# Two of four parts of the difference tables ahead of the first relu, products on plain tables first, and state stores ahead of weights, in the second layer of a graph network

## The reference, cut to what matters

```python
def conv(h, W, b):
    h = h @ W
    agg = jax.ops.segment_sum(h[src] * norm, dst, num_segments=n)
    return agg + b
h = jnp.maximum(_layernorm(x, axis=-1), 0.0)
h = jax.nn.relu(conv(h, W1, b1))
h = jax.nn.relu(conv(h, W2, b2))          # the "second layer" of the title
x = x + conv(h, W3, b3)
h = jnp.maximum(_layernorm(x, axis=-1), 0.0)
msg = h[edge_src] + relvectors[edge_rel]
red = jax.ops.segment_sum(msg, edge_dst, num_segments=h.shape[0])
x = x + _gru_cell(red, h, w_ih, w_hh, b_ih, b_hh)
```

## Time and profile before

| | |
|---|---|
| median of three runs | 869.26 us |
| the profiled execution | 868.13 us, of which its span is 864.0 us |
| mean granted TensorE clock | 0.987 of full |
| PE busy | 823.6 us (95%) |
| DVE, ACT, POOL busy | 606.2, 297.5 and 117.0 us |

### The profile page before, as it was taken

How to read it: one execution, slowest core, us unless ns; L and a number is a source line. 1 busy time by engine, 2 the same in 40 slices (tenths; PEclk the granted TensorE clock), 3 DMA queues, 4 the chain that set the end, 5 groups by cost and what they waited for, 6 DMA issues and landing times.

```text
span 864.0 us, 14285 instructions
## 1 busy us (share of the span) xinstructions
PE 823.6 (95%) x4710; PEld 466.9 (54%) x4710; DVE 606.2 (70%) x1319; ACT 297.5 (34%) x604; POOL 117.0 (14%) x244
## 2 busy tenths in 40 slices
PE   2889999999999996999999999999999999999997
PEld 1357566666666444455545545555554555455554
DVE  8945999999999277253869546575664746565677
ACT  3365666776766222110101212221302122112233
POOL 0210110012000046555730000000000000000000
PEclk9889999999999998999999999999999999999999
DMA  6100000000000512332111112222705112111232
GB/s 205 33 2 1 4 18 23 17 17 17 24 17 17 172 38 76 111 75 75 40 35 55 53 55 85 74 86 79 214 3 163 32 42 51 31 36 42 57 79 53
DMA packets 83769, 49.83 MB, mean 58 GB/s; under 512 B 46667, under 2 KB 80220, under 8 KB 83692
## 3 DMA queue, kind: packets, MB, share of 16 engines
q1 hardware_dynamic: 73836, 39.00, 16.1%
q10 hardware_dynamic: 9856, 9.85, 3.6%
HBM read 29.68 MB, written 18.78 MB: 56 GB/s over the span
## 4 chain that ended last, share of the span: by engine, by line
PE 83%; DVE 11%; issue 2%; DMA 2%; ACT 1%; SPq 1%; ACTq 0%; DVEq 0%
PE ps L1396 16%; PE ps L1058 13%; PE ps L1743 9%; PE ps L1570 8%; PE ps L955 8%; PE ps L757 5%; PE ps L764 5%; PE ps L1421 5%; PE ps L1439 3%; PE ps L769 2%; PE ps L774 2%; PE ps L1030 2%; DVE node_b L298 1%; DVE count L598 1%; PE ps L986 1%
## 5 line engine op out<-in xcount | busy, mean ns | idle before, releaser
L1058 PE MATMUL ps<-node_a,count 128*128 128x512 f16 x525 | 181.1, 381 | 1.5 <-DVE node_a L1165 1.0
L955 PE MATMUL ps<-node_b 128*128 128x175 f16 x808 | 162.3, 256 | 6.7 <-DVE node_b L298 5.3
L298 DVE TENSOR_TENSOR node_b<-node_b 128x1024 f16<-128x1024 f16 (+2 forms) x253 | 157.3, 670 | 0.0
L1254 ACT ACTIVATE count<-ps 128x500 f32 x202 | 122.8, 608 | 65.2 <-PE ps L955 59.5
L1396 PE MATMUL ps<-count,node_a 128*128 128x512 f16 (+2 forms) x686 | 130.7, 351 | 0.0
L955 PEld LDWEIGHTS ps<-node_b 128*128 128x128 f16 x808 | 79.5, 100 | 36.0 <-issue 6.2
L2327 POOL TENSOR_TENSOR count<-count,node_a 16x20 f16 x202 | 86.1, 426 | 92.8 <-DMA chapter_starts<-in_dst 52.3
L1396 PEld LDWEIGHTS ps<-count,node_a 128*128 128x128 f16 (+1 forms) x686 | 60.1, 98 | 69.1 <-issue 0.4
L1743 PE MATMUL ps<-count,node_a 128*128 128x512 f16 x288 | 64.1, 379 | 0.0
L1058 PEld LDWEIGHTS ps<-node_a,count 128*128 128x128 f16 x525 | 53.2, 101 | 18.9 <-ACT count L1254 1.2
L1701 DVE TENSOR_TENSOR count<-count 128x6144 f16<-128x6144 f16 x14 | 46.9, 3353 | 17.6 <-PE ps L1570 16.3
(11 more groups left out here) (289 smaller groups left out, 1137.2 us busy)
## 6 DMA issues: line engine op xcount, KB each, us to landing
node_a<-second_scratch ACTq DMA_DIRECT2D x6, 768.0 KB, 4.3
node_a<-in_x SPq DMA_DIRECT2D x4, 768.0 KB, 8.4
second_scratch<-node_a ACTq DMA_DIRECT2D x4, 768.0 KB, 3.5
state_scratch<-params SPq DMA_DIRECT2D x24, 128.0 KB, 1.9
node_b<-state_scratch SPq DMA_DIRECT2D x96, 32.0 KB, 2.1
table_scratch<-agg SPq DMA_DIRECT2D x21, 128.0 KB, 1.8
mixed_scratch<-node_b SPq DMA_DIRECT2D x10, 256.0 KB, 2.0
node_a<-mixed_scratch SPq DMA_DIRECT2D x4, 640.0 KB, 6.8
```

The lines of the kernel that those rows point to most:

```text
L298: return DVE.tensor_tensor(to, iota, keys.unsqueeze(2).to_broadcast([P, n, width, 2]), ALU.is_equal)
L955: return PE.matmul(window(s)[:, :, keys], low, key_hot[k][:, j, :, i].rearrange("p (t w) -> p t w", w=SPAN), start=(s == 0 and j == 0), st ...
L1058: last = PE.matmul(out_slot(u)[0:m, :], count[:, t, u * P:u * P + m], node_a[:, t, :, :].rearrange("p a d -> p (a d)"), start=(t == 0), st ...
L1254: ACTE.activation(to, window(s), ACT.Copy).then_inc(win_written, 1)
```

## The change

It has three pieces. In the second layer, two of the four parts of the difference tables are made before the first relu of chunk 0 and two after it (before: three and one), and the step s1 of pair 2 moves behind the relu of chunk 6. A pair's products come in the order B21, B11, T1, T4, T2, B22, T3, with T4 in bank 3 and the separate tail in bank 0; DVE makes s4 right after s2, both after T1, and in pair 2 the steps y, a12 and a21 of pair 1 come ahead of c11 and s2. Tables are placed and loaded otherwise: four go into `node_b`, where two did. At the end of the third layer, SP stores the state of the last chunk's first two tiles ahead of its wait and of the loads of weights.

```diff
-        SECOND_PRODUCTS = (T1, B21, B11, T4, T2, B22, T3)
-        TAKEN, ADDED = ("t1", "c11", "c21"), ("c11", "c12", "tail", "b22", "c21", "c22")
+        SECOND_PRODUCTS = (B21, B11, T1, T4, T2, B22, T3)
+        TAKEN, ADDED = ("c11", "t1", "c21"), ("c11", "c12", "tail", "b22", "c21", "c22")
@@ second_place @@
-            if p == 1:
-                return slot(SLOT_P if which in (T1, T2) else SLOT_Q)
-            if which in (T1, T2):
+            if (p, which) in ((1, T1), (1, T3), (2, T4)):
                 return slot(SLOT_P)
-            f = 1 if which == T4 else 0
-            return node_b[:, 0:T - 1:2, :, f * P:(f + 1) * P]
+            if (p, which) == (1, T4):
+                return slot(SLOT_Q)
+            odd, f = (1, 0) if (p, which) == (2, T2) else (0, 1)
+            return node_b[:, odd:T - 1:2, :, f * P:(f + 1) * P]
...
-        SECOND_BANK = {T1: 0, T4: 0, B21: 1, B22: 1, B11: 2, T2: 2, T3: 2}
-        TAIL_SUMS = 3
+        SECOND_BANK = {T1: 0, T4: 3, B21: 1, B22: 1, B11: 2, T2: 2, T3: 2}
+        TAIL_SUMS = 0
@@ second_sums_pe @@
-            PE.wait_ge(*SECOND_IN[p, T1])
-            PE.wait_ge(*second_step_at("s1", p))
             if p == 1:
-                PE.wait_ge(sums_out, 4)
+                PE.wait_ge(sums_out, 5)
             else:
-                PE.wait_ge(*second_taken_at(p - 1, "c21"))
-            second_product_pe(p, T1, True, None).then_inc(product_done, 1)
+                PE.wait_ge(*second_added_at(p - 1, "b22"))
+            second_product_pe(p, B21, True, (0, 0)).then_inc(product_done, 1)
             if p == 1:
                 convs_pe(1, 0, 2)
             else:
                 half_convs_pe(p - 1, 1)
-                PE.wait_ge(*second_added_at(p - 1, "b22"))
-            second_product_pe(p, B21, True, (0, 0)).then_inc(product_done, 1)
+            second_product_pe(p, B11, True, None).then_inc(product_done, 1)
+            PE.wait_ge(*SECOND_IN[p, T1])
+            PE.wait_ge(*second_step_at("s1", p))
             if p > 1:
-                PE.wait_ge(*second_added_at(p - 1, "c22"))
-            second_product_pe(p, B11, True, None).then_inc(product_done, 1)
-            second_tail_pe(p, ps[:, TAIL_SUMS, :], 1, 1, True)
+                PE.wait_ge(*second_added_at(p - 1, "tail"))
+            second_product_pe(p, T1, True, None).then_inc(product_done, 1)
             PE.wait_ge(*SECOND_IN[p, T4])
+            if p > 1:
+                PE.wait_ge(*second_taken_at(p - 1, "c21"))
+            second_product_pe(p, T4, True, (0, 1))
             PE.wait_ge(*second_taken_at(p, "t1"))
-            second_product_pe(p, T4, True, (0, 1)).then_inc(product_done, 1)
+            second_tail_pe(p, ps[:, TAIL_SUMS, :], 1, 1, True).then_inc(product_done, 1)
@@ layers_dve @@
-            for b in range(2):
-                parts_dve(b)
-                second_step_dve("s1", b + 1)
-                parts_low_dve(b)
-            parts_dve(2)
-            parts_low_dve(2)
-            relu_chunk(PLAIN[0])
-            parts_dve(3)
-            parts_low_dve(3)
-            relu_chunk(PLAIN[1])
+            parts_dve(0)
+            second_step_dve("s1", 1)
+            parts_low_dve(0)
+            parts_dve(1)
+            parts_low_dve(1)
+            relu_chunk(PLAIN[0])
+            for b in (2, 3):
+                parts_dve(b)
+                parts_low_dve(b)
+            relu_chunk(PLAIN[1])
+            second_step_dve("s1", 2)
             for p in PAIRS_OUT:
+                relu_chunk(PLAIN[2] if p == 1 else 2 * p - 1)
+                if p == 2:
+                    for which in ("y", "a12", "a21"):
+                        second_step_dve(which, 1)
+                second_add_dve(p, "c11")
                 second_step_dve("s2", p)
-                relu_chunk(PLAIN[2] if p == 1 else 2 * p - 1)
                 second_step_dve("s4", p)
...
@@ layers_act @@
-            for b in (1, 2):
-                parts_high_act(b)
-                parts_store_act(b)
+            parts_high_act(1)
+            parts_store_act(1)
             sums_of(0, 1)
             highs(PLAIN[0])
             for f in range(HALVES):
                 sums_of(1, f)
-            parts_high_act(3)
-            parts_store_act(3)
+            for b in (2, 3):
+                parts_high_act(b)
+                parts_store_act(b)
             sums_of(2, 0)
...
@@ layers_sp @@
+            for t in tiles_of[chunks[-1]][:2]:
+                state_store_sp(order, place[t])
             SP.wait_ge(*product_at(0, B22))
             SP.wait_ge(*step_at(0, "s3"))
             gru_weights_sp()
...
-            for t in tiles_of[chunks[-1]]:
+            for t in tiles_of[chunks[-1]][2:]:
                 state_store_sp(order, place[t])
```

More of the change, by code:

```diff
@@ L1510, in program @@
         PLAIN, PAIRS_OUT = chunks[:3], (1, 2)
-        SECOND_PRODUCTS = (T1, B21, B11, T4, T2, B22, T3)
-        TAKEN, ADDED = ("t1", "c11", "c21"), ("c11", "c12", "tail", "b22", "c21", "c22")
-        SECOND_STEPS = [("s1", 1), ("s1", 2), ("s2", 1), ("s4", 1), ("s3", 1), ("s2", 2), ("s4", 2), ("y", 1), ("a12", 1), ("a21", 1),
+        SECOND_PRODUCTS = (B21, B11, T1, T4, T2, B22, T3)
+        TAKEN, ADDED = ("c11", "t1", "c21"), ("c11", "c12", "tail", "b22", "c21", "c22")
+        SECOND_STEPS = [("s1", 1), ("s1", 2), ("s2", 1), ("s4", 1), ("s3", 1), ("y", 1), ("a12", 1), ("a21", 1), ("s2", 2), ("s4", 2),
                         ("s3", 2), ("y", 2), ("a12", 2), ("a21", 2)]
@@ L1541, in second_table @@
             return second_place(p, which)[:, i, part, :]
-        SECOND_IN = {(1, T1): (nodes_in[0], 32), (1, T2): (nodes_in[0], 48), (2, T1): (nodes_in[0], 64), (2, T2): (nodes_in[0], 80),
-                     (1, T4): (nodes_in[1], 32), (1, T3): (nodes_in[1], 48), (2, T4): (nodes_in[2], 48), (2, T3): (nodes_in[3], 48)}
+        SECOND_IN = {(1, T1): (nodes_in[0], 32), (1, T3): (nodes_in[0], 48), (2, T4): (nodes_in[0], 64), (1, T4): (nodes_in[1], 32),
+                     (1, T2): (nodes_in[2], 48), (2, T1): (nodes_in[2], 80), (2, T3): (nodes_in[2], 112), (2, T2): (nodes_in[3], 48)}
         PART_ORDER = (T1, T3, T4, T2)
@@ L1669, in second_load_act @@
             of = second_dram[PART_ORDER.index(which), :, :].rearrange("p (i a d) -> p i a d", a=2, d=P)
-            if (p, which) in ((2, T4), (2, T3)):
+            if SECOND_IN[p, which][0] in nodes_in[2:]:
                 for part in range(2):
@@ L1697, in second_step_dve @@
             else:
-                DVE.wait_ge(*second_product_at(p, {"s2": T1, "s4": B21, "s3": T2}.get(which, T3)))
+                DVE.wait_ge(*second_product_at(p, {"s2": T1, "s4": T1, "s3": T2}.get(which, T3)))
             if n:
@@ L2148, in layers_act @@
             sums_of(2, 1)
-            second_load_act(2, T4)
+            second_load_act(1, T2)
             for p in PAIRS_OUT:
-                second_take_act(p, "t1")
-                second_load_act(p, T2)
-                highs(PLAIN[2] if p == 1 else 2 * p - 1)
                 second_take_act(p, "c11")
                 if p == 2:
-                    ACTE.wait_ge(*second_product_at(p, B11))
-                    second_load_act(p, T3)
+                    second_load_act(p, T2)
+                highs(PLAIN[2] if p == 1 else 2 * p - 1)
+                second_take_act(p, "t1")
+                second_load_act(p, T3)
                 second_take_act(p, "c21")
                 if p == 1:
-                    second_load_act(p, T3)
                     ACTE.wait_ge(*second_product_at(p, T2))
                     second_load_act(p + 1, T1)
+                    ACTE.wait_ge(*second_product_at(p, T3))
+                    second_load_act(p + 1, T4)
                 highs(2 * p)
```

## The result

The changed kernel takes 857.81 us (median of four, 857.42 to 858.21); before, it is 868.6 us (median of four, 866.5 to 869.59). The ratio is 0.9879, with a 95% interval of 0.9858 to 0.9900: 1.2% faster. The forecast was 859.2 us. The profiled execution took 857.42 us, with a span of 853.2 us against 864.0.

A forecast was written before the change was run, and what follows sets the result against it. PE, busy 95%, was taken as the bound, with two waits from 300 to 700 us. Gains 6.80 + 2.08 + 1.86 less a new 0.70 wait make 10.04 us off the 869.26 median: 859.2 us, range 857.6 to 862.8.

The forecast's parts named there:

- The wait for `agg`: Before the second layer's first convs: PE no longer waits for ACT's copy of the second sum, gain 6.80 us.
- The convs' clock: First 16 convs: without idle time PE's clock stays up, 3.45 us instead of 5.53, gain 2.08 us.
- The cover of parts 2 and 3: Pair 1's first product B21: the moved parts and fifth copy finish about 5 us before PE wants them, no wait.
- The wait at T2 of pair 2: DVE's chain of relu, three steps, c11 and s2 ends late, so PE waits 0.7 us before T2.
- The stores: End of third layer: earlier state stores free DVE's transpositions, so PE's tail no longer waits for t3, gain 1.86 us.
- Sum: Whole kernel: 6.80 + 2.08 - 0.70 + 1.86 = 10.04 us off the profiled execution, median expected 859.2 us.
- Rival 1: Before T2 of pair 2: PE's wait is 1 to 3.4 us larger, 860.2 to 862.6 us; chance 0.12.
- Rival 2: At B21 of pair 1: parts 2 and 3 come late, about 1 us wait plus 2 for clock, 862.2 us; chance 0.04.
- Rival 3: End of third layer: the moved state stores bring nothing, 1.86 us not gained, 861.1 us; chance 0.05.
- rival 5: At the first convs: PE still waits as before, so no change, 868 us; chance 0.04.
- rival 4: DVE steps before T2 of pair 2: POOL holds each 3.17 us longer, slower at 871.9 us; chance 0.03.
- 1.1 us for steps that come second to POOL: Five DVE steps in pair 2, each blocked by a 0.22 us POOL instruction: 860.3 us, left out of the total.

The follow-up runs named there:

- the first piece alone: Kernel before with only the difference-table parts split two and two and s1 of pair 2 later: 861.79 us, ratio 0.9933.
- the other two pieces alone: Kernel before with only the new order of products, steps, banks and tables: 868.32 us; kernel before with only the earlier state stores: 865.18 us.
- the piece alone: Kernel before with only the stores of the first two state tiles moved ahead of the weights: 865.18 us, ratio 0.9974.

## Why the prediction was right

- **The wait for `agg`.** Forecast 6.80 us, measured 29.68 - 22.86 = 6.82. The kernels with part 2 behind the copy lack the wait (the change, the one with a21 later, the first piece alone); before and the other two pieces alone, with part 2 ahead, show 6.6 to 6.7.
- **The convs' clock.** Forecast 2.08, measured 5.53 - 3.54 = 1.99; the first convs after a sum take 0.09 more than later ones, which I had taken as the measure.
- **The cover of parts 2 and 3.** Forecast that B21 would wait for nothing; the fifth copy was over at 350.37 + 0.69 = 351.06 and B21 started at 356.03, with the 5 us of cover that were forecast. Forecast 8.88 in sum up to B21, measured 8.81.
- **The wait at T2 of pair 2.** Forecast 0.70, measured 0.85. Relu and steps took their rows' lengths: 407.61 to s2's end at 427.16 is 19.55, as from 408.5 to 428.05 in the forecast. Of the 0.15 that was missing, 0.09 is that T2 starts that much after s2's end, and 0.05 that the relu began 1.06 after the convs and not 1.01. The changed kernel's other two traces have 0.80 and 0.86 here. Moving a21 took the wait away, so the cause is shown.
- **The stores.** Forecast 1.86. In the change the tail follows without idle time, which is the whole 1.86, and the piece alone gave 2.09 with 0.25 of it from the clock elsewhere.
- **Sum.** Forecast 10.04 off the profiled execution; the traces give 8.81 - 0.85 + 1.86 = 9.82 from the first sums on, and 9.81 is the difference of the rests. The other 0.99 of the 10.8 us between the spans lies before and is that stage's own spread. The medians lie 10.8 apart, that of the changed kernel 1.4 under the forecast: 0.7 of that is before's own median, which is 868.6 with a fourth run, and the rest is no larger than the spread between the three pairs of medians (10.8, 10.0, 8.5). So the forecast was right by its terms, which the traces bear out one by one, and the times alone, whose gains spread over more than 2 us, couldn't have told it from 9 or 11 us.
- **The rivals.** Rival 1 was right in its place and not in its size. Rival 2's cover held. Rival 3 fell with the piece alone, and rival 5 with the wait for `agg` gone. For rival 4 the steps after took 3296 to 3397 ns, at most 24 ns more than before, with POOL at work beside most of them:

```profile
L1702 DVE TENSOR_TENSOR count<-count x14: 3296/3358/3397, 312.4 to 462.8; 128x6144 f16<-128x6144 f16 x14
```

In all twelve traces together the 168 steps took 3294 to 3406 ns, so no step waited even the 0.22 us of one POOL instruction. One such instruction began at 412.87, 0.03 us ahead of the first of the three steps at 412.90, and they took 10.32 us, 0.04 more than in the trace with a21 later (10.28 for three). The prediction's 1.1 us for steps that come second to POOL counts five steps; only four stand ahead of T2, so the price would have been 4 x 0.22 = 0.88 and its time 860.1, not 860.3.

What the prediction lacked is a reason for the second piece. It costed each piece against the others as they stand, found 0.7 us of loss for the order of products, and did not ask what the first piece does without it: 4.04 us less in the trace. It also did not say that ACT's copy of c11 now stands ahead of chunk 1's high halves and waits there for the convs, first on ACT, then on DVE:

```profile
365.36 0.69 ACT L1686 ACTIVATE agg<-ps,scales 128x512 f32<-128x512 f32 x1 [8.44 <-PE ps L1421]
...
366.38 0.43 DVE L1920 TENSOR_TENSOR node_a<-pair_a,node_a 128x256 f16<-128x256 f32 x1 [2.33 <-ACT node_a L2111]
```

DVE stood idle for that, which cost nothing, as T1's end and not DVE set the start of s2 in pair 1.

## What to carry to other kernels

When the busiest engine has two waits left, its list of waits, a start-to-start sum on its timeline and the lists of the engines ahead of each wait gave the gain of three edits within 0.3 us of what the traces show. Ask of each edit also what it is worth without the others, since one that only costs may be the cover of another's gain. Moving a block out of the way of a copy pays at the place that waits, and the block has to be followed to the next thing that stands behind it. Where steps are put in a row ahead of one that a product waits for, count their pitch (3.46 us here, not 3.36), and let each that nobody waits for go behind it.

## What the runs showed of the hardware that I had not expected

An idle PE can cost more than its idle time, and not in proportion: 1.69 us in front of the convs cost 1.80 in all, which is the wait alone (1.85 from start to start), but 3.12 us cost 5.05, and 2.18 us in front of T1 cost 4.04, with a granted clock of 0.50, the 1.2 GHz level, in the stretch from 360 to 362 us of that trace. After the 0.68 us in front of T2 it stayed at 1.00. A longer wait did not always cost more clock: the convs took 5.96 us after 6.01 us of idle time and 5.28 and 5.53 after 6.65. The stage ahead of the second layer, which no run changes, ends at 305.06 to 307.48 us, and later the lower the granted clock of its first 100 us is (0.97 to 0.89). And a pause that the profile lists under "issue" was a wait for a DVE step: moving one step took it away.
